# Two layers over a dense 8192 x 8192 adjacency on one core: x in another DMA queue, one-time work in other places, high and low G summed in the same columns

## The chip, the core and the metric

One core of a Trainium2 chip runs the program once. The metric is the device time in microseconds (us), from start to end of the program, lower is better. The engines are TensorE (PE), VectorE (DVE), ScalarE (ACT), GpSimd (POOL) and SyncE (SP); each works through its own list of instructions in order and waits on semaphores for the others. 16 DMA engines move data between HBM and the core's memory.

## What is computed

Two graph layers with a residual and a layer norm each, over N = 8192 nodes with F = 64 features. adj is a float32 matrix of 8192 x 8192 (268 MB) that holds only 0 and 1.

```python
def _L0_gnn_ref(X, adj, W, b):
    deg = jnp.clip(jnp.sum(adj, axis=1, keepdims=True) + 1.0, 1.0, None)
    h_neigh = (adj @ X + X) / deg
    z = jnp.concatenate([X, h_neigh], axis=1) @ W + b
    out = jax.nn.relu(z)
    norm = jnp.linalg.norm(out, axis=1, keepdims=True)
    return out / jnp.maximum(norm, 1e-12)

def _L1_gnn_ref(features, adj, W):
    deg = jnp.sum(adj, axis=1, keepdims=True)
    neigh = adj @ features / (deg + 1.0)
    return jnp.concatenate([features, neigh], axis=-1) @ W.T

x = _layernorm(x + _L0_gnn_ref(x, adj, L0_gnn_W, L0_gnn_b), axis=-1)
x = _layernorm(x + _L1_gnn_ref(x, adj, L1_gnn_W), axis=-1)
```

The second layer needs adj @ features, and these features are the first layer's result.

## The kernel before

**The stream.** adj is read once. It goes through in 64 row blocks n of 128 rows, each in four chunks c of 128 x 2048 float32 (1 MB). `a_in` has R = 6 buffers for them. SyncE issues chunk t = 4n + c as soon as VectorE (`s_e`) and ScalarE (`s_half`) are done with chunk t - 6. With each chunk:

- VectorE compares it with 1.0 into 8-bit codes `e8` (`compare`, L802).
- ScalarE sums the upper halves of its words, as a check that there are only zeros and ones (`sum_codes`, L589). The first use of ScalarE loads its table.
- TensorE multiplies the codes, as pairs in float16, with powers of two (`pack_chunk`, L371), which transposes them and packs eight rows' bits into a byte. ScalarE takes the packed bytes to `pk` (`take_packed`), GpSimd keeps copies in `store` (`keep`), VectorE unpacks them into `t_sb`, fp8 weights of 0 or 2 (`unpack`, L809).
- TensorE sums: for each of the 64 column blocks b, the weights `t_sb[b]` times a row of `xh`, into `s_ps` (`sum_quarter`, L385).

**What `xh` holds.** For each column block 257 columns in float16: g high (64) and g low (64), which are the first layer's results as two halves, x high (64), x low (64), and a constant for the degree (1). The columns of g are known only for the column blocks whose first layer is done. `lows(n)` says how many of these row block n uses: 0 up to row block 10, then 8, 16, 24, 32, 40 for eight row blocks each, 48 from row block 51 on. For b < lows(n) the matmul has all 257 columns, for the others the last 129. What a row block missed is made up from `store`: in pieces beside the stream (`unpack_piece`, `catch_up` L404, `add_piece`, from row block 12 on), and the last 16 column blocks for all rows after the stream (`unpack_tail`, `tail_sums` L466 and L470, `add_tail`).

**The first layer.** Every four row blocks (a group e) ScalarE has copied the sums into `agg` (`take_sums`, L609: 257 columns or 129). GpSimd adds x low to x high (`join_x`, L1186) and g low to g high (`join_g`), and copies the degrees to `dcol`. VectorE divides by the degree (`mean`, L847 and L851), and then come transposes, the dense product, `norm`, `residual`, `normalise`, the second dense product, `low_part` and `begin_acc`, over row blocks 4e + 5 to 4e + 7, on all engines in turn.

**One-time work.** x comes in four DMAs from ScalarE's queue (L577), behind the weights. `split_x(q)` makes a quarter of x high on ScalarE and of x low on VectorE, one after each chunk of row block 1. `weights()` (L765 to L780) and `bias()` (L785 to L794) run on VectorE at the end of row block 2. `guard_x(q)` (L759, L760) checks the squares of a quarter of x, in row blocks 3 to 6. `verdict()` uses them at the very end.

**The order** is written out by hand: each engine has one loop over n, in which the calls stand between the four chunks. VectorE's, shortened:

```python
for n in range(NB):
    compare(n, 0)
    if n: unpack(n - 1, 0)
    ...
    compare(n, 3)
    if n == 2:
        weights()
        bias()
    if 3 <= n < 7:
        guard_x(n - 3)
```

## Time and profile before

| | |
|---|---|
| median of 3 runs | 761.63 us (760.83 to 764.16) |
| the profiled execution | 762.74 us |
| its span, first to last instruction | 760.9 us |
| PE, DVE, ACT, POOL busy | 83%, 90%, 77%, 41% of the span |
| mean granted TensorE clock | 0.948 of full speed |
| read from HBM | 270.60 MB, 358 GB/s over the span |

A time in a row counts from the span's start. "Busy" is the time in which an engine works on an instruction; TensorE's matmuls overlap, so its busy share is no measure of its peak. The granted clock is TensorE's share of full speed: 1.00 is 2.4 GHz, 0.50 is 1.2 GHz, and a stretch between the two is a mixture. "Idle before <- releaser" says for what an engine waited. The chain is followed back from the last instruction, at each step to what released it. The DMA share is the mean of the 16 DMA engines.

### The profile page before, as it was taken

The page shows a single profiled execution, that of the slowest core. Times are in us where ns is not written, and L with a number is a line of the kernel's source. Part 1 is how long each engine was busy: PE and PEld are TensorE (multiplying, and loading weights), DVE is VectorE, ACT ScalarE, POOL GpSimd, SP SyncE. Part 2 cuts the span into 40 slices and gives each one's busy share as a digit, 9 for nine tenths or more (in the row PEclk, how much of TensorE's full clock was granted, in tenths as well). Part 3 has the DMA queues.
Part 4 walks back from the last instruction along what each step waited for, and adds up shares of the span by engine and source line. Part 5 has one row for each costly group of instructions (what it writes and reads, how often), then busy time and mean ns, then how long its engine had stood idle before and what let it go on. Part 6 is the DMA issues. An engine that isn't in the chain of part 4 may idle for free.

```text
span 760.9 us, 27768 instructions
## 1 busy us (share of the span) xinstructions
PE 630.8 (83%) x11125; PEld 580.0 (76%) x11125; DVE 682.1 (90%) x2506; ACT 588.8 (77%) x815; POOL 312.3 (41%) x360
## 2 busy tenths in 40 slices
PE   1357687687777778979899998999999999998994
PEld 0246677676776677878788887989898989988994
DVE  4499998989998999899999999999999999987895
ACT  1978879989898888989889898888898888850021
POOL 0233323433421425664354545556553546341025
PEclk9987877989999997999999999999999999999998
DMA  9999999999999999999999999999999999900003
GB/s 361 406 366 402 420 347 420 422 420 418 421 419 419 419 419 407 382 419 419 419 414 420 408 421 402 420 413 408 413 391 420 399 418 394 420 24 2 2 18 102
DMA packets 41516, 274.54 MB, mean 361 GB/s; under 512 B 4455, under 2 KB 8615, under 8 KB 8615
## 3 DMA queue, kind: packets, MB, share of 16 engines
q1 hardware_dynamic: 39040, 270.55, 87.1%
q10 hardware_dynamic: 2342, 2.16, 0.9%
q8 instruction: 90, 1.47, 0.8%
q14 instruction: 44, 0.35, 0.1%
HBM read 270.60 MB, written 2.10 MB: 358 GB/s over the span
## 4 chain that ended last, share of the span: by engine, by line
PE 31%; DVE 25%; issue 13%; ACT 11%; DMA 11%; POOL 7%; ACTq 2%; DVEq 0%; POOLq 0%; SPq 0%
PE s_ps L385 17%; DMA a_in<-in_adj 11%; ACT junk L589 8%; DVE e L802 7%; DVE t_sb L809 6%; PE u_ps L404 5%; POOL small L1179 4%; PE p_ps L371 2%; PE z_ps L454 2%; DVE q_sb L870 2%; DVE y_sb L864 2%; ACTq L577 2%; PE p_ps L466 1%; DVE a_in L809 1%; POOL store L1211 1%
## 5 line engine op out<-in xcount | busy, mean ns | idle before, releaser
L589 ACT ACTIVATE junk<-a_in 128x2048 uint8<-128x2048 uint16 x256 | 488.4, 1913 | 8.8 <-DMA a_in<-in_adj 8.6
L385 PE MATMUL s_ps<-xh,t_sb 128*128 128x129 f16 x4096 | 388.2, 251 | 52.3 <-DVE t_sb L809 48.8
L385 PEld LDWEIGHTS s_ps<-xh,t_sb 128*128 128x128 fp8e4 x4096 | 314.7, 103 | 81.3 <-DVE t_sb L809 53.8
L802 DVE TENSOR_SCALAR e<-a_in 128x2048 uint8<-128x2048 f32 x256 | 314.1, 1234 | 18.7 <-DMA a_in<-in_adj 17.9
L1211 POOL COPY store<-pk 128x32 uint32<-128x32 uint32 (+1 forms) x250 | 176.1, 746 | 179.9 <-ACT pk L598 179.9
L809 DVE TENSOR_SCALAR t_sb<-pk 128x128 uint32<-128x128 uint32 x1024 | 159.1, 227 | 5.6 <-ACT pk L598 4.8
L371 PE MATMUL p_ps<-pow_h,e 128*128 128x16 f16 x2048 | 90.8, 171 | 65.7 <-DVE e L802 55.0
L371 PEld LDWEIGHTS p_ps<-pow_h,e 128*128 128x128 f16 x2048 | 77.6, 99 | 79.9 <-DVE e L802 60.1
L1179 POOL TENSOR_TENSOR small<-small,minus_half 128x4 f32<-128x4 f32 x32 | 68.8, 2150 | 151.8 <-DVE small L858 104.9
L404 PE MATMUL u_ps<-xh,u_sb 128*128 128x64 f16 x2976 | 105.6, 192 | 0.0
L404 PEld LDWEIGHTS u_ps<-xh,u_sb 128*128 128x128 fp8e4 x2976 | 100.6, 97 | 1.2
L1186 POOL TENSOR_TENSOR agg<-agg 128x256 f32<-128x256 f32 x16 | 30.5, 1905 | 74.1 <-ACT agg L609 74.1
L809 DVE TENSOR_SCALAR u_sb<-store 128x128 uint32<-128x128 uint32 (+5 forms) x416 | 58.6, 213 | 0.0
L598 ACT ACTIVATE pk<-p_ps 128x256 uint16<-128x256 f32 x128 | 47.9, 374 | 9.1 <-PE p_ps L371 9.1
L589 ACT ACTIVATION_READ_ACCUMULATOR junk<-a_in 128x1 f32 x256 | 50.6, 198 | 0.0
L615 ACT COPY cat_t<-c_ps 128x512 f32<-128x512 f32 x16 | 9.4, 585 | 31.1 <-PE c_ps L418 31.1
L633 ACT COPY h_t<-c_ps 64x512 f32<-64x512 f32 x16 | 9.3, 579 | 29.1 <-PE c_ps L446 29.1
L1218 POOL TENSOR_TENSOR fvar<-fvar,minus_half 128x8 f32<-128x8 f32 x8 | 16.1, 2012 | 37.9 <-DVE fvar L940 37.1
L609 ACT COPY agg<-s_ps 128x257 f32<-128x257 f32 (+1 forms) x64 | 22.5, 352 | 6.6 <-PE s_ps L388 6.6
L809 DVE TENSOR_SCALAR a_in<-store 128x256 uint32<-128x256 uint32 x128 | 26.9, 285 | 0.0
L652 ACT ACTIVATE t_sb<-xl 128x512 f32<-128x512 f32 x7 | 4.4, 626 | 28.6 <-DVE xl L929 28.6
L639 ACT CAST xh<-z_ps 128x256 f16<-128x256 f32 x16 | 6.0, 372 | 22.2 <-PE z_ps L454 22.1
(119 smaller groups left out, 487.5 us busy)
## 6 DMA issues: line engine op xcount, KB each, us to landing
a_in<-in_adj SPq DMA_DIRECT2D x256, 1024.0 KB, 11.2
xl<-in_x ACTq DMA_DIRECT2D x4, 512.0 KB, 18.3
out_h<-e SPq DMA_DIRECT2D x8, 256.0 KB, 2.1
b_sb<-in_L_gnn_b ACTq DMA_DIRECT2D x3, 0.2 KB
w_sb<-in_L_gnn_W ACTq DMA_DIRECT2D x1, 32.0 KB
w_raw<-in_L_gnn_W ACTq DMA_DIRECT2D x1, 32.0 KB
```

The lines of the kernel that those rows point to most:

```text
L371: last = nc.tensor.matmul(p_ps[:, c // 2, at:at + PK], e_pair[:, c, u // 2, :, u % 2], pow_h[:, :], start=True, stop=True)
L385: last = nc.tensor.matmul(s_ps[:, n % 2, at:GW], t_sb[:, b // 2, b % 2::2], xh[:, b, at:GW], start=(b == 0), stop=False)
L404: last = nc.tensor.matmul(u_rows[:, r, 0:F], u_sb[:, (r * W + b) // 2, b % 2::2], xh[:, low(q - 1) + b, part * F:(part + 1) * F], start=(b ...
L589: nc.scalar.activation(junk[:, t % 2, :], halves[t % R], ACT.Copy, scale=1.0 / 128, accum_out=half_sum[:, n, c:c + 1]).then_inc(s_half, 1)
L598: nc.scalar.activation(pk_u[:, n % 2, h * 256:(h + 1) * 256], p_ps[:, h, 0:256], ACT.Copy, bias=-CODE_SUM, scale=1024.0).then_inc(s_pk, 1)
L609: nc.scalar.copy(agg[:, e % 2, k, at:GW], s_ps[:, n % 2, at:GW]).then_inc(s_agg, 1)
L802: nc.vector.tensor_scalar(e8[:, c, :], a_in[:, t % R, :], 1.0, float(CODE), ALU.is_equal, ALU.add).then_inc(s_e, 1)
L809: ins = nc.vector.tensor_scalar(plane(g), src, by, BIT4, op, ALU.bitwise_and)
L1179: nc.gpsimd.tensor_tensor(small[:, dst, :], small[:, src, :], minus_half[:, 0:BR], ALU.pow).then_inc(s_root, 1)
L1186: nc.gpsimd.tensor_tensor(hi, hi, lo, ALU.add).then_inc(s_xsum, 1)
L1211: ins = nc.gpsimd.tensor_copy(stored(s, n, 1), pk_w[:, n % 2, at:at + WIDTH[s] * PKW])
L1218: nc.gpsimd.tensor_tensor(fvar[:, 1, rows], fvar[:, 1, rows], minus_half[:, :], ALU.pow).then_inc(s_froot, 1)
```

## The change

- SyncE issues x, behind the four chunks of row block 0; ScalarE no longer does.
- ScalarE makes a copy of one column into `warm` before its first chunk; its table load goes there.
- `split_x` for all four quarters, and ScalarE's `take_weights`, stand ahead of row block 1's first chunk. `weights()` goes to the end of row block 1, `bias()` behind the second chunk of row block 0 (with a wait for the weight DMAs), the guards to row blocks 20, 24, 28 and 32.
- A known column block is summed by two matmuls with the same weights: g high (64 columns) into columns 0 to 63 of `s_ps`, then g low, x high, x low and degree (193 columns) into columns 0 to 192. So g high and g low add up in PSUM, and the sum is 193 columns wide instead of 257. The first column block takes three. `agg` and `take_sums` become narrower.
- GpSimd's `join_x` and `join_g` go. VectorE adds x low to x high in `mean`. GpSimd keeps the copy to `dcol` (`keep_degrees`). `begin_acc` no longer waits for it.

```diff
+GUARD = [20, 24, 28, 32]
...
+                if n == 0:
+                    for q in range(NC):
+                        sp.dma_start(x_in[:, q * CB:(q + 1) * CB, :].rearrange("p (j r) f -> p j (r f)", r=IL),
+                                     x_j[:, q * CB // IL:(q + 1) * CB // IL, :]).then_inc(s_x[q], 16)
...
                 for b in range(i * CB, (i + 1) * CB):
-                    at = 0 if b < lows(n) else HP
-                    last = nc.tensor.matmul(s_ps[:, n % 2, at:GW], t_sb[:, b // 2, b % 2::2], xh[:, b, at:GW],
-                                            start=(b == 0), stop=False)
+                    row_bits = t_sb[:, b // 2, b % 2::2]
+                    if b < lows(n):
+                        nc.tensor.matmul(s_ps[:, n % 2, 0:F], row_bits, g_hi[:, b, :], start=(b == 0), stop=False)
+                    if 0 < b < lows(n):
+                        last = nc.tensor.matmul(s_ps[:, n % 2, 0:SW], row_bits, xh[:, b, F:GW], start=False, stop=False)
+                        continue
+                    if b < lows(n):
+                        nc.tensor.matmul(s_ps[:, n % 2, 0:F], row_bits, g_lo[:, b, :], start=False, stop=False)
+                    last = nc.tensor.matmul(s_ps[:, n % 2, F:SW], row_bits, xh[:, b, HP:GW],
+                                            start=(b == 0 and not lows(n)), stop=False)
...
-            for q in range(NC):
-                act.dma_start(x_in[:, q * CB:(q + 1) * CB, :].rearrange("p (j r) f -> p j (r f)", r=IL),
-                              x_j[:, q * CB // IL:(q + 1) * CB // IL, :]).then_inc(s_x[q], 16)
+            act.wait_ge(s_const, 1)
+            nc.scalar.copy(warm[:, :], ident[:, 0:1])
...
-                at = 0 if lows(n) else HP
-                nc.scalar.copy(agg[:, e % 2, k, at:GW], s_ps[:, n % 2, at:GW]).then_inc(s_agg, 1)
+                at = 0 if lows(n) else F
+                nc.scalar.copy(agg[:, e % 2, k, at:SW], s_ps[:, n % 2, at:SW]).then_inc(s_agg, 1)
...
             def bias():
 
+                dve.wait_ge(s_w, 80)
...
-                dve.wait_ge(s_xsum, e + 1)
+                hi, lo = (agg[:, par, :, F + i * F:2 * F + i * F] for i in range(2))
+                link(nc.vector.tensor_tensor(hi, hi, lo, ALU.add))
...
-            def join_x(e):
+            def keep_degrees(e):
...
                 pool.wait_ge(s_agg, (e + 1) * BR)
-                hi, lo = (agg[:, e % 2, :, HP + i * F:HP + (i + 1) * F] for i in range(2))
-                nc.gpsimd.tensor_tensor(hi, hi, lo, ALU.add).then_inc(s_xsum, 1)
...
-                    nc.gpsimd.tensor_tensor(hi, hi, lo, ALU.add)
```

VectorE at the start of the program, before. L802 is a chunk's comparison, L752 a quarter of x low, L809 an unpacking of eight instructions, L765 the first instruction of the weights:

```order
L752 SCALAR_TENSOR_TENSOR xh<-xl,xh 128x16x64
L802 TENSOR_SCALAR e<-a_in 128x2048
L809 TENSOR_SCALAR t_sb<-pk 128x16x8 x8
L802 TENSOR_SCALAR e<-a_in 128x2048 x2
L809 TENSOR_SCALAR t_sb<-pk 128x16x8 x8
L802 TENSOR_SCALAR e<-a_in 128x2048
L765 TENSOR_TENSOR w_sb<-w_sb,ident 64x64
L766 TENSOR_REDUCE small<-w_sb 128x1
L767 TENSOR_SCALAR small<-small 128x1
L768 TENSOR_TENSOR w_sb<-w_sb,small 128x64
```

The same place in the changed kernel, where the lines are L811, L760 and L818. L803 is the last instruction of the bias, L773 the first of the weights:

```order
L803 CAST b_rows<-b_sum 3x256
L811 TENSOR_SCALAR e<-a_in 128x2048 x2
L760 SCALAR_TENSOR_TENSOR xh<-xl,xh 128x16x64 x4
L811 TENSOR_SCALAR e<-a_in 128x2048
L818 TENSOR_SCALAR t_sb<-pk 128x16x8 x8
L811 TENSOR_SCALAR e<-a_in 128x2048 x2
L818 TENSOR_SCALAR t_sb<-pk 128x16x8 x8
L811 TENSOR_SCALAR e<-a_in 128x2048
L773 TENSOR_TENSOR w_sb<-w_sb,ident 64x64
L774 TENSOR_REDUCE small<-w_sb 128x1
```

The bias now ends ahead of row block 0's last two comparisons, and the four quarters of x low stand together ahead of row block 1. The weights follow row block 1 instead of row block 2.

SyncE's first rows in the changed kernel (before, all 256 chunks stand in one row):

```order
L329 UNCONDITIONAL_BRANCH
L337 DMA a_in<-in_adj 128x2048 x4
L340 DMA xl<-in_x 128x4x256 x4
L337 DMA a_in<-in_adj 128x2048 x252
L348 DMA out_h<-e 128x2x256 x8
```

Four DMAs of x now stand between chunk 3 and chunk 4.

TensorE in row block 12, at the first sums that know g (row block 11, lows = 8), before. L371 packs a chunk, L385 sums:

```order
L385 MATMUL s_ps<-xh,t_sb 128x129 x16
L388 MATMUL s_ps<-xh,id 128x129
L371 MATMUL p_ps<-pow_h,e 128x16 x8
L385 MATMUL s_ps<-xh,t_sb 128x257 x8
L385 MATMUL s_ps<-xh,t_sb 128x129 x8
L371 MATMUL p_ps<-pow_h,e 128x16 x8
```

And in the changed kernel, the same place (L378 packs, L393 to L399 sum):

```order
L402 MATMUL s_ps<-xh,id 128x129
L378 MATMUL p_ps<-pow_h,e 128x16 x8
L393 MATMUL s_ps<-xh,t_sb 128x64
L398 MATMUL s_ps<-xh,t_sb 128x64
L399 MATMUL s_ps<-xh,t_sb 128x129
L393 MATMUL s_ps<-xh,t_sb 128x64
L395 MATMUL s_ps<-xh,t_sb 128x193
L393 MATMUL s_ps<-xh,t_sb 128x64
```

A matmul of 257 columns became one of 64 and one of 193, and the first of the row block three.

## Rows read from the trace of the kernel before

**Rows 1.** The page, part 2: DMA share and GB/s in 40 slices.

```profile
DMA  9999999999999999999999999999999999900003
GB/s 361 406 366 402 420 347 420 422 420 418 421 419 419 419 419 407 382 419 419 419 414 420 408 421 402 420 413 408 413 391 420 399 418 394 420 24 2 2 18 102
```

**Rows 2.** Waits of SyncE's own queue: who, for whom, us, times, longest.

```profile
SPq L333 <- ACT junk L589: 505.5, 243, 15.7
```

**Rows 3.** The line of SyncE's chunk issues (L334): from issue to landing.

```profile
DMA to landing us min/median/max: 4.7/11.2/16.8
```

**Rows 4.** Windows: length, busy us of each engine, granted clock, DMA share, GB/s.

```profile
52.00:58.00 6.00, 2.91 (x38) 2.82 (x39) 5.86 (x19) 0.48 (x4) 0.00 (x0) 0.50 0.70 249
58.00:66.00 8.00, 5.99 (x82) 5.73 (x80) 7.93 (x20) 8.00 (x11) 1.99 (x6) 0.71 1.05 420
66.00:70.00 4.00, 3.94 (x68) 3.77 (x66) 4.00 (x11) 3.12 (x5) 1.56 (x3) 0.77 0.89 324
70.00:96.00 26.00, 16.05 (x230) 14.61 (x227) 25.62 (x74) 21.31 (x31) 10.97 (x18) 0.85 1.01 422
96.00:116.00 20.00, 16.84 (x233) 15.50 (x234) 18.67 (x55) 15.99 (x21) 3.19 (x16) 0.77 0.98 350
...
120.00:300.00 180.00, 140.10 (x2249) 126.12 (x2248) 166.00 (x635) 160.23 (x218) 62.12 (x124) 0.91 1.01 418
300.00:490.00 190.00, 172.52 (x3131) 158.26 (x3130) 179.35 (x675) 166.10 (x226) 102.59 (x93) 0.98 1.01 413
```

**Rows 5.** The same for four row blocks near the stream's end.

```profile
615.00:656.00 41.00, 40.16 (x684) 36.57 (x682) 38.53 (x147) 35.49 (x49) 20.69 (x10) 1.00 1.00 407
```

**Rows 6.** The chain that ended last, 675:705: start, us, what.

```profile
679.32 6.27 PE s_ps L385 x64
...
686.11 3.75 PE u_ps L466 x64
689.86 0.44 PE c_ps L418 x4
690.30 3.57 PE p_ps L466 x64
```

**Rows 7.** Timeline of VectorE, 44:56: start, us, engine, line, operation.

```profile
45.64 0.21 DVE L765 TENSOR_TENSOR w_sb<-w_sb,ident 64x64 f32<-64x64 f32 x1
...
49.24 0.17 DVE L785 MEMSET ones_bf<- 3x128 bf16 x1
...
53.12 1.21 DVE L802 TENSOR_SCALAR e<-a_in 128x2048 uint8<-128x2048 f32 x1
```

**Rows 8.** Groups by line, VectorE, 20:130: the guards' two instructions.

```profile
L760 DVE TENSOR_REDUCE xsq<-store 128x16 f32<-128x1024 f32 x4 | 4.9, 1220 | 0.1
L759 DVE TENSOR_TENSOR store<-xl 128x1024 f32<-128x1024 f32 x4 | 4.8, 1211 | 0.0
```

**Rows 9.** Timeline of all engines, 0:20.

```profile
3.15 13.10 ACTq L577 DMA_DIRECT2D xl<-in_x  x4
...
5.86 1.23 DVE L802 TENSOR_SCALAR e<-a_in 128x2048 uint8<-128x2048 f32 x1 [1.78 <-DMA a_in<-in_adj]
...
16.29 1.28 ACT L589 ACT_TABLE_LOAD   x1 [16.29 <-issue]
...
17.58 1.91 ACT L589 ACTIVATE junk<-a_in 128x2048 uint8<-128x2048 uint16 x1
```

**Rows 10.** The chain that ended last, 629:640.

```profile
631.30 1.43 PE u_ps L404 x48
...
634.11 1.80 PE s_ps L385 x16
...
637.06 0.92 PE s_ps L385 x16
```

**Rows 11.** Timeline of GpSimd and VectorE, 648:655.

```profile
648.90 2.50 POOL L1186 TENSOR_TENSOR agg<-agg 128x256 f32<-128x256 f32 x1 [2.61 <-ACT agg L609]
...
651.50 0.43 DVE L851 TENSOR_TENSOR cat_in<-agg,small 128x256 f32<-128x256 f32 x1 [0.60 <-DVE small L847]
```

## What I expected before it ran

> **What bounds the kernel now.** I read the page first, then the share and rate of the DMA over the span, then windows of it, then the chain.
>
> The adjacency is 268 MB and has to come through once, so the first thing to see is the DMA line: it stands at 9 in 35 of 40 slices, and its GB/s line is about 420 in most of them but 366, 402, 347 and 383 in some [rows 1]. Until the last megabyte has landed the kernel can't end sooner than the stream lets it. So an engine that is made faster is worth nothing there, unless it was late enough to leave the queue empty. Only six chunks of a_in exist; SyncE sends the next one when VectorE and ScalarE are both done with the one six before, and a chunk takes 11.2 us from issue to landing in the median [rows 3], so there are normally more than four in the queue. SyncE's 505.5 us of waiting for ScalarE [rows 2] is therefore no loss in itself: that wait is how a full queue looks. A loss is a window in which the rate drops.
>
> The windows show where it does [rows 4]. From 120 to 300 us the rate is 418 GB/s, which I take as what the stream gives. It is 249 in 52:58, 324 in 66:70 and 350 in 96:116. The time lost is (418 - 249) / 418 x 6 = 2.4 us, (418 - 324) / 418 x 4 = 0.9 us and (418 - 350) / 418 x 20 = 3.3 us, 6.6 us together. Before 52 us there is a short dip while x itself comes, 2 MB in small packets, and these are still sent after the change. After 120 us nothing of this size is left.
>
> In the last third a second bound comes up beside the stream. In 615:656 TensorE is busy for 40.16 of 41 us, at the full granted clock, with the DMA still at 407 GB/s; VectorE is busy for 38.53 and ScalarE for 35.49 [rows 5]. The two bounds are level there. After the stream the end hangs on TensorE's sums of row block 63, then on its tail sums [rows 6].
>
> **The early edits: what they give.** The loss in 52:58 has one cause that the rows show. VectorE works on the weights from 45.64 and on the bias from 49.24, and takes its next chunk only at 53.12, so one-time work of 7.4 us stands between two chunks [rows 7]. Then come four guards of 1.21 + 1.22 = 2.43 us each, 9.7 us together, in row blocks 3 to 6 [rows 8]. VectorE is busy for 7.93 of 8 us in 58:66, for 4.00 of 4 in 66:70 and for 25.62 of 26 in 70:96 [rows 4]. It has no room to catch up: 17.1 us of one-time work lie where each microsecond makes TensorE and ScalarE late too.
>
> The change takes the bias (53.12 - 49.24 = 3.9 us) into row block 0, between the second chunk and the third. VectorE waits there for each chunk anyway (1.78 us before the first, [rows 9]), and has one comparison of 1.23 us to do in the 2.5 us of a chunk. The weights (3.6 us) go to the end of row block 1, and the guards to row blocks 20, 24, 28 and 32. VectorE is busy for 166.00 of 180 us in 120:300 and for 179.35 of 190 in 300:490 [rows 4]: 14.0 and 10.7 us are free, and two guards, 4.9 us, are put into each. A row block is four chunks of 2.5 us, and a guard makes one chunk 2.4 us late where there are four in the queue. So I cost the moved guards at nothing; the cover is the queue, and if it is gone each guard costs up to 2.4 us.
>
> ScalarE's early start goes the same way. Its issues of x held it until 16.25 us, then came the table load of 1.28 us, and its first chunk began at 17.58 though VectorE had taken it at 5.86 [rows 9]. After the change it takes chunk 0 as it lands, some 12 us earlier. In row block 1 both engines now wait for all of x before they take a chunk; in SyncE's queue x stands behind four chunks, so the last of its bytes moves at 1 + 6.3 MB / 0.418 = 16 us or, its packets being small, a few us later, and chunk 4 stands behind it. Both engines are therefore ready when chunk 4 lands. The copy into warm and the table load lie in idle time. The bytes are the same, so x itself gives and costs 0.
>
> How much of the 6.6 us comes back? The 2.4 and the 0.9 us follow VectorE's 17.1 us and I take them whole. In 96:116 the granted clock is 0.77, a mixture of the two levels, and TensorE is busy for 16.84 of 20 us [rows 4]: it slows down after it idled behind VectorE, and some of this belongs to the first dense stage and stays. Of the 3.3 us I take 1.9. Sum: **-5.2 us**. The bounds are -2.4 us (only 52:58 is mended) and -6.6 us (all of it).
>
> **The sums in the same columns.** A known column block of a row block was one matmul of 257 columns, and is now one of 64 and one of 193 with the same weights, loaded twice (for the first block three: 64, 64, 129). The chain gives what one takes in a row at full clock: 1.80 / 16 = 112.5 ns for 257 columns, 0.92 / 16 = 57.5 ns for 129, 1.43 / 48 = 29.8 ns for 64 [rows 10]. No row has 193; on the line between 129 and 257 it is 57.5 + 64 x 55 / 128 = 85.0 ns. The pair takes 114.8 ns, 2.3 more than before. lows(n) is 8, 16, 24, 32, 40 for eight row blocks each from 11 on, and 48 for the 13 row blocks from 51: 1584 pairs, 3.6 us of TensorE in all. Up to row block 50 the stream hides it. From 51 on TensorE and the stream are level, so 13 x 48 = 624 pairs stand on the path: 624 x 2.3 ns = **+1.4 us**, and the 13 first blocks add 13 x 5 ns = 0.1 us. Bounds: 0, if the 0.84 us in 41 that TensorE idles take it up [rows 5]; above, 55.8 ns (3.57 / 64) for the short one, as a matmul of 128 columns with its own weights takes [rows 6], so 26 ns more on each of 624, +16 us. I take the value of the 64-column row, because L404 does just this: two matmuls of 64 columns with the same weights one after the other, into the same columns.
>
> Here the Trainium skill speaks against the change. TensorE: Matmul & The Clock Gate, section Back-to-back issue gap, gives about 81 ns a matmul as the sustained rate of 128 columns with weight loads, because both operations set the spacing. By it a pair would take at least 162 ns. The rows have 55.8 ns for that shape [rows 6] and 29.8 ns for 64 columns [rows 10], so the trace does not agree, and the sum goes by the rows; with 162 ns the 624 pairs would cost 49.5 ns each, 31 us.
>
> **What this takes from the others.** GpSimd's join of x took 2.50 us in the stream; VectorE was idle for 0.60 us before L851, which needs it [rows 11]. Now VectorE adds 256 elements itself, about 0.43 us like L851, plus the link: 0.1 us less than the wait. GpSimd also loses the join of G; what is queued behind the two (keep, then root) only starts earlier, 0. ScalarE's copy of s_ps is 193 columns instead of 257, and ScalarE has 5.5 us free in 41 [rows 5]: 0. begin_acc loses its wait for dcol: 0. In the tail TensorE sums row block 63 in 6.27 us, 0.1 more with 48 pairs (counted above), and the shorter copy behind it gives 0.1 back; the earlier mean is swallowed, since TensorE's tail sums are in front of the transposes [rows 6].
>
> **Sum.** The profiled execution took 762.74 us, its span 760.9; the median of the runs is 761.63. Change: -5.2 + 1.5 - 0.1 for the mean = -3.8, less 0.2 kept for the waits on x in row block 1, so -3.6 us. Span 757.3, that execution 759.1, the median **758.0 us**. One can tell 0.5% (3.8 us) from no change here, and this is just under it.
>
> **Rivals.**
> *All of it comes back.* The late engines in 96:116 are only the echo of VectorE's 17.1 us, and TensorE's idle takes up the pairs: 761.6 - 6.6 = 755.0. For it: VectorE had no microsecond free from 58 to 96. Against: the clock of 0.77 in a stretch whose work stays. Chance 0.17.
> *The dips move.* Row blocks 4 to 9 stay irregular, the clock stays low, and only 52:58 is mended; TensorE pays at the end: -2.4 + 1.5 = -0.9, 760.7. Chance 0.18.
> *The short matmul pays for its weights.* Place: TensorE from row block 51, where it is level with the stream. It decides the sign at 5.2 us / 624 = 8 ns on a pair. At the upper bound of 28 ns it is +17.5 - 5.2 = +12.3, 774 us, and it would start earlier than row block 51, so rather more. For it: the weights of a short one have only 27 ns of columns to hide behind. Against: 29.8 ns on 48 in a row. Chance 0.10.
> *x in SyncE's queue does not do what it should.* ScalarE's four issues took 13.10 us [rows 9]. SyncE's may be held too, with chunks 4 and 5 behind it. At the least one quarter of x, 0.5 MB or 1.3 us, is then left to move, and a chunk lands 4.7 us after its issue at the least [rows 3], so up to 3.4 us would be lost: 761.4. Against: the queue holds six megabytes by then, and an issue is let through as packets end. Chance 0.06.
>
> **How the numbers follow.** The forecast has 0.49; it spans 755.5 to 760.5, and half of it lies under 757.8. Faster by over 0.5%: 0.25 + 0.17 = 0.42. Within: 0.24 + 0.18 + 0.06 + 0.02 of the short matmul's small prices = 0.50. Slower: 0.08. The range is 754.5 to 762.5: it takes in all but the short matmul's prices.
>
> **What would show it.** Windows of the changed kernel: 415 to 420 GB/s in each from 24 to 120 us, VectorE with idle time in 58:96, and no fall in 200:340, where the guards went (right); a dip of 250 or 350 left in 96:116 (second rival). The chain in the last 100 us: a 64 and a 193 matmul should start 115 ns apart from the next pair (right), 125 or more is the third rival. Row block 51 should come 5 us earlier than before, row block 63's sums 3.6 us earlier; if the first holds and the second doesn't, TensorE's price was mis-sized. The whole is wrong if the stream stops being the bound before row block 51.

## The result and the profile after

The changed kernel takes **772.64 us** in the median of its runs (771.15 to 773.74); the kernel before, run beside it, 762.59 (760.83 to 764.16). The ratio is 1.013, 95% interval 1.010 to 1.016: slower by 10 us, where I had forecast 758.0. The profiled span is 770.9, before 760.9.

The page of the changed kernel, part 2, DMA share and GB/s in 40 slices of 19.3 us, and its line of the instruction packets from part 3 (packets, MB, share of 16 engines):

```profile
DMA  9999999999999999999999999999999999900003
GB/s 346 420 422 419 420 417 421 418 421 415 420 419 419 416 408 397 418 402 403 411 403 408 397 420 403 392 372 369 380 405 390 396 387 392 379 8 2 3 18 99
...
q8 instruction: 102, 1.67, 0.9%
```

The beginning is what the change was for: no slice from the second to the fourteenth is under 415, where [rows 1] has 366, 402 and 347. The end is new: from slice 25 on the rate is 369 to 405, where before it was 391 to 420. The same in windows (length, busy us of PE, PEld, DVE, ACT, POOL with counts, granted clock, DMA share, GB/s), the first five against [rows 4]:

```profile
52.00:58.00 6.00, 4.64 (x78) 4.21 (x77) 3.54 (x10) 5.03 (x8) 0.00 (x0) 0.87 1.01 419
58.00:66.00 8.00, 4.97 (x71) 4.43 (x69) 6.49 (x20) 6.78 (x9) 2.48 (x8) 0.79 1.01 420
66.00:70.00 4.00, 2.23 (x43) 1.79 (x40) 2.74 (x7) 3.95 (x6) 2.05 (x7) 1.00 1.02 424
70.00:96.00 26.00, 21.55 (x255) 19.44 (x256) 23.00 (x83) 22.24 (x33) 11.63 (x18) 0.71 1.01 420
96.00:116.00 20.00, 13.66 (x207) 12.06 (x205) 15.87 (x48) 17.90 (x24) 3.74 (x16) 0.84 1.01 418
```

```profile
533.00:574.00 41.00, 39.24 (x854) 38.44 (x854) 36.82 (x139) 35.56 (x49) 19.33 (x10) 1.00 0.95 369
574.00:615.00 41.00, 40.15 (x840) 39.07 (x838) 37.43 (x147) 34.59 (x48) 16.43 (x8) 1.00 0.99 395
615.00:656.00 41.00, 38.50 (x829) 37.68 (x827) 35.73 (x135) 33.21 (x47) 16.76 (x8) 1.00 0.99 391
```

In the late windows no engine is busier than before. In 615:656 TensorE has 38.50 us of work where [rows 5] has 40.16, VectorE 35.73 for 38.53, ScalarE 33.21 for 35.49, and the stream is slower too. Everybody waits for somebody. The groups of TensorE in 492:656 say for whom; line, shape and count, busy us and mean ns, then the idle time before them and who ended it. First of the kernel before, then of the changed one:

```profile
L385 PE MATMUL s_ps<-xh,t_sb 128*128 128x257 f16 (+1 forms) x1018 | 107.7, 257 | 2.6 <-DVE t_sb L809 2.6
L404 PE MATMUL u_ps<-xh,u_sb 128*128 128x64 f16 x1200 | 41.1, 192 | 0.0
```

```profile
L395 PE MATMUL s_ps<-xh,t_sb 128*128 128x193 f16 x665 | 84.0, 247 | 1.1 <-issue 1.0
L393 PE MATMUL s_ps<-xh,t_sb 128*128 128x64 f16 x681 | 83.0, 193 | 2.2 <-DVE t_sb L818 1.2 <-issue 1.0
L418 PE MATMUL u_ps<-xh,u_sb 128*128 128x64 f16 x1136 | 39.3, 192 | 1.9 <-issue 1.8
L399 PE MATMUL s_ps<-xh,t_sb 128*128 128x129 f16 x304 | 23.5, 219 | 1.6 <-issue 1.6
```

Before, TensorE never stood still for "issue", that is with nothing to wait for in the profile. After the change it did for 5.4 us here. The timeline of TensorE shows what such a piece looks like:

```profile
530.99 0.62 PE L399 MATMUL s_ps<-xh,t_sb 128*128 128x129 f16 x8
531.45 1.21 PE L418 MATMUL u_ps<-xh,u_sb 128*128 128x64 f16 x35
534.04 0.55 PE L418 MATMUL u_ps<-xh,u_sb 128*128 128x64 f16 x13 [1.38 <-issue]
534.42 0.35 PE L378 MATMUL p_ps<-pow_h,e 128*128 128x16 f16 x8
```

48 matmuls of catch_up should run without a break: nothing is waited for between them, and before the change they took 1.43 us [rows 10]. Here 35 go, TensorE stands for 1.38 us, and 13 follow. The break is in the middle of a loop body whose operands were all there.

One more column of the trace fits it. The queue named "instruction" brings packets of 16 KB through the same 16 DMA engines as adj; there were 90, now there are 102. One of them started at 531.6, 0.9 us before that break. I counted the breaks of this kind between 120 and 690 us: two matmuls of one run (the same line, or the two lines of a pair) that start more than 330 ns apart. The kernel before has none. The changed kernel has 15, 13.8 us in all from start to start, and each begins 0.3 to 2.0 us after the start of an instruction packet, while such a packet starts every 6.2 us in 492:656. That made the first theory.

Where time was gained and lost, as the start of VectorE's comparison of a row block's first chunk against the kernel before (us, from the trace):

```
row block            12    28    36    44    48    52    56    60    63
changed kernel     -6.3  -7.1  -4.3  -2.4  -0.4  +3.7  +4.5  +6.3  +8.8
```

The chain that ended last has its last long piece of sums, then the tail, as in [rows 6]:

```profile
693.85 0.91 PE s_ps L399 x16
695.23 3.75 PE u_ps L480 x64
699.42 3.57 PE p_ps L480 x64
```

686.11 has become 695.23, 9.1 us later; the tail behind it has the same length to within 0.9 us.

### The profile page after: what moved, and what is told of

Its sections match the earlier page's. It is cut to its first block, busy times and chain, and to the rows that moved or that the text cites. A ratio compares the mean times of both kernels' runs of the same rounds, so it can differ in the third digit from the quotient of the medians.

```text
span 770.9 us, 31027 instructions
## 1 busy us (share of the span) xinstructions
PE 645.1 (84%) x12762; PEld 615.8 (80%) x12762; DVE 681.2 (88%) x2522; ACT 588.1 (76%) x816; POOL 290.6 (38%) x330
## 4 chain that ended last, share of the span: by engine, by line
PE 40%; DVE 21%; DMA 13%; issue 13%; ACT 7%; POOL 3%; SPq 1%; ACTq 0%; DVEq 0%; POOLq 0%
DMA a_in<-in_adj 13%; PE s_ps L395 11%; PE u_ps L418 7%; PE s_ps L399 6%; ACT junk L602 5%; DVE e L811 5%; DVE t_sb L818 5%; PE s_ps L393 5%; PE p_ps L378 3%; POOL small L1182 2%; PE z_ps L468 2%; DVE q_sb L880 2%; DVE y_sb L874 2%; PE p_ps L480 1%; DVE a_in L818 1%
## 5 line engine op out<-in xcount | busy, mean ns | idle before, releaser
L602 ACT ACTIVATE junk<-a_in 128x2048 uint8<-128x2048 uint16 x256 | 488.4, 1913 | 17.3 <-DMA a_in<-in_adj 17.0
L811 DVE TENSOR_SCALAR e<-a_in 128x2048 uint8<-128x2048 f32 x256 | 311.7, 1224 | 23.8 <-DMA a_in<-in_adj 23.0
L1205 POOL COPY store<-pk 128x32 uint32<-128x32 uint32 (+1 forms) x250 | 198.6, 836 | 228.9 <-ACT pk L611 228.9
L399 PE MATMUL s_ps<-xh,t_sb 128*128 128x129 f16 x2565 | 204.9, 235 | 23.5 <-DVE t_sb L818 19.4
L393 PE MATMUL s_ps<-xh,t_sb 128*128 128x64 f16 x1584 | 200.2, 196 | 18.9 <-DVE t_sb L818 14.7
L395 PE MATMUL s_ps<-xh,t_sb 128*128 128x193 f16 x1531 | 200.1, 252 | 1.1 <-issue 1.0
L399 PEld LDWEIGHTS s_ps<-xh,t_sb 128*128 128x128 fp8e4 x2565 | 171.6, 105 | 26.3 <-DVE t_sb L818 21.9
L393 PEld LDWEIGHTS s_ps<-xh,t_sb 128*128 128x128 fp8e4 x1584 | 153.0, 99 | 21.5 <-DVE t_sb L818 16.6
L818 DVE TENSOR_SCALAR t_sb<-pk 128x128 uint32<-128x128 uint32 x1024 | 152.2, 222 | 5.5 <-ACT pk L611 4.7
L395 PEld LDWEIGHTS s_ps<-xh,t_sb 128*128 128x128 fp8e4 x1531 | 153.0, 100 | 2.1 <-issue 1.3
L378 PE MATMUL p_ps<-pow_h,e 128*128 128x16 f16 x2048 | 91.6, 171 | 65.5 <-DVE e L811 61.8
L1182 POOL TENSOR_TENSOR small<-small,minus_half 128x4 f32<-128x4 f32 x32 | 65.9, 2060 | 200.8 <-DVE small L868 152.1
L378 PEld LDWEIGHTS p_ps<-pow_h,e 128*128 128x128 f16 x2048 | 77.6, 99 | 79.2 <-DVE e L811 68.8
L818 DVE TENSOR_SCALAR u_sb<-store 128x128 uint32<-128x128 uint32 (+5 forms) x416 | 59.7, 218 | 0.0
L849 DVE TENSOR_TENSOR xl<-u_ps,xl 128x256 f32<-128x256 f32 (+5 forms) x52 | 20.3, 391 | 10.0 <-PE u_ps L418 10.0
```

The lines of the kernel that those rows point to most:

```text
L378: last = nc.tensor.matmul(p_ps[:, c // 2, at:at + PK], e_pair[:, c, u // 2, :, u % 2], pow_h[:, :], start=True, stop=True)
L393: nc.tensor.matmul(s_ps[:, n % 2, 0:F], row_bits, g_hi[:, b, :], start=(b == 0), stop=False)
L395: last = nc.tensor.matmul(s_ps[:, n % 2, 0:SW], row_bits, xh[:, b, F:GW], start=False, stop=False)
L399: last = nc.tensor.matmul(s_ps[:, n % 2, F:SW], row_bits, xh[:, b, HP:GW], start=(b == 0 and not lows(n)), stop=False)
L602: nc.scalar.activation(junk[:, t % 2, :], halves[t % R], ACT.Copy, scale=1.0 / 128, accum_out=half_sum[:, n, c:c + 1]).then_inc(s_half, 1)
L811: nc.vector.tensor_scalar(e8[:, c, :], a_in[:, t % R, :], 1.0, float(CODE), ALU.is_equal, ALU.add).then_inc(s_e, 1)
```

## The experiments

**Theory A:** TensorE runs out of instructions; with more of them per microsecond, its packets come too late beside the stream. **Theory B:** the second matmul of a pair costs because it adds into columns that the one ahead has just written. A third candidate was the early edits themselves. I split the change in two and took 1488 matmuls away in another place.

**The early edits alone.** The changed kernel with the sums, agg and the joins as they were before; against the changed kernel:

```diff
-                    if b < lows(n):
-                        nc.tensor.matmul(s_ps[:, n % 2, 0:F], row_bits, g_hi[:, b, :], start=(b == 0), stop=False)
-                    if 0 < b < lows(n):
-                        last = nc.tensor.matmul(s_ps[:, n % 2, 0:SW], row_bits, xh[:, b, F:GW], start=False, stop=False)
...
+                    last = nc.tensor.matmul(s_ps[:, n % 2, at:GW], t_sb[:, b // 2, b % 2::2], xh[:, b, at:GW],
+                                            start=(b == 0), stop=False)
```

> The kernel before with the early edits alone (x's loads in SyncE's queue, warm-up of ScalarE, splits of x before the compares, guards and bias moved); sums as before: one matmul of 257 columns per known row block, joins on GpSimd. The kernel before has a median of 762.6 us, the changed one 772.6. Theory A (TensorE runs short of instructions: the loss comes with the number of its instructions) and theory B (the loss comes from adding into columns that the matmul ahead has just written) both say that the early gain stays: 757 us (756 to 758.5), since in the changed kernel chunk (13,0) landed 5.9 us and chunk (40,0) 5.8 us earlier than before. If the early edits are what spoils the late row blocks (the rival here), it is 762 or more.

760.26 us (757.71 to 763.23), ratio 0.997 [0.9952, 0.9989], span 757.9. The rule for breaks finds one pause of 0.4 us, at 131 us; it lies 11 us behind a packet and so is of another kind.

**The same-column sums alone.** The other half of the change; against the changed kernel:

```diff
-GUARD = [20, 24, 28, 32]
...
-                        split_x(q)
-                    take_weights()
...
+                if n == 1:
+                    split_x(0)
...
+                if 3 <= n < 7:
+                    guard_x(n - 3)
```

> The kernel before with the same-column sums alone (64 + 193 columns, joins moved from GpSimd to VectorE); the early part as before. If the two halves of the change add up, its time is the changed kernel's plus the early gain: 772.6 + 5.5 = 778 us (775 to 780). If the loss only exists because the stream of adj runs ahead by 5 us, it is 763 to 767.

772.35 us (771.23 to 774.55), ratio 1.0128 [1.0103, 1.0153], span 771.1, with 15 breaks, 11.4 us (one of them, 0.4 us at 138 us, is 11 us behind a packet). So the loss comes with the sums, and the two halves do not add up: the early edits are worth 2 to 3 us by themselves and nothing beside the sums. My 778 took the early gain for 5.5 us at the end; with 2.4 us, what the early edits give alone, it would have been 775, and the rest of the miss is that the halves do not add up.

**Fewer matmuls in catch_up.** In the changed kernel:

```diff
-                        for part in range(2):
-                            last = nc.tensor.matmul(u_rows[:, r, 0:F], u_sb[...], xh[:, low(q - 1) + b, part * F:(part + 1) * F],
-                                                    start=(b + part == 0), stop=(b + part == W))
+                        last = nc.tensor.matmul(u_rows[:, r, :], u_sb[...], xh[:, low(q - 1) + b, 0:HP],
+                                                start=(b == 0), stop=(b == W - 1))
...
+                link(nc.vector.tensor_tensor(rows, u_rows[:, 0:r1 - r0, 0:F], rows, ALU.add))
+                nc.vector.tensor_tensor(rows, u_rows[:, 0:r1 - r0, F:HP], rows, ALU.add).then_inc(s_uadd, 1)
```

> The changed kernel with the products of the stored codes merged: one matmul of 128 columns (high and low part side by side) in place of two of 64 columns that add up in the same columns, and one more addition on VectorE per row block from 12 on. 1488 matmuls and as many weight loads fewer. The main sums keep their same-column form. Theory A: the gaps of TensorE that wait for nothing fall from 15 us to under 6, and with two of 64 columns at 31.5 ns each giving way to one at 57.5 it comes to 760 us (757 to 764). Theory B as far as the main sums go: their pairs cost what they did, the merged ones save 5.5 ns x 1488 = 8 us of TensorE at most: 765 to 768 us, gaps as in the changed kernel.

768.51 us (767.26 to 770.01), ratio 1.0073 [1.0051, 1.0095]. The breaks are gone: none between 120 and 690, with 8709 matmuls there, the main sums still in their pairs into the same columns. That speaks for A. The time only fell by 4 us, and A had promised 12. The likely reason, VectorE, comes further down.

**The same number of instructions, no column written twice.** In the kernel with the early edits alone:

```diff
+                    row_bits = t_sb[:, b // 2, b % 2::2]
                     at = 0 if b < lows(n) else HP
-                    last = nc.tensor.matmul(s_ps[:, n % 2, at:GW], t_sb[:, b // 2, b % 2::2], xh[:, b, at:GW],
-                                            start=(b == 0), stop=False)
+                    if b < lows(n):
+                        nc.tensor.matmul(s_ps[:, n % 2, 0:HP], row_bits, xh[:, b, 0:HP], start=(b == 0), stop=False)
+                        at = HP
+                    last = nc.tensor.matmul(s_ps[:, n % 2, at:GW], row_bits, xh[:, b, at:GW],
+                                            start=(b == 0 and not lows(n)), stop=False)
```

> e1_early (760.3 us; 757.9 in its profiled span) with each 257-column matmul of a known row block sent as two, of 128 and 129 columns, that write different columns: as many instructions on TensorE as the changed kernel, no column written twice; ScalarE, VectorE and GpSimd as in e1_early. Theory A (TensorE runs short of instructions above some rate): gaps over 330 ns inside runs of one line, 11 to 14 us of them between 120 and 690 (changed kernel 13.8, early edits alone 0.4), each 1 to 2 us behind a packet of the instruction queue, and 770 us (767 to 774). Theory B (adding into columns just written costs): no such gaps, 760 to 763 us.

769.21 us (768.35 to 770.0), ratio 1.0091 [1.0074, 1.0108], 13 breaks, 9.6 us, each 1.1 to 2.3 us behind a packet's start. Theory B had 760 to 763. It falls: 9 of the 12 us between the early edits alone and the changed kernel are there without a column that is written twice. TensorE's groups of this kernel in 492:656:

```profile
L396 PE MATMUL s_ps<-xh,t_sb 128*128 128x129 f16 x986 | 105.5, 220 | 2.2 <-issue 2.2
L394 PE MATMUL s_ps<-xh,t_sb 128*128 128x128 f16 x699 | 86.2, 219 | 1.5 <-DVE t_sb L815 1.4
L415 PE MATMUL u_ps<-xh,u_sb 128*128 128x64 f16 x1136 | 39.3, 192 | 0.8 <-issue 0.7
```

**Half the dose.** The same with `if b < lows(n) and b % 2:`.

> e3_split2 with the odd column blocks alone split: half the extra instructions. About 9450 matmuls between 120 and 690 beside 8700 (early edits alone; no gaps) and 10150 (changed kernel; 13.8 us of gaps). Theory A in its form with a threshold (packets of 16 KB that come at their own pace): fewer than 5 us of gaps and a span of 760 to 763; if the loss is in proportion to the instructions: 6 to 7 us of gaps and a span of 764. Theory B: no gaps, span 758 to 759.

One execution: span 760.0, 9451 matmuls between 120 and 690, one break of 0.3 us. The breaks are no straight line in the number of matmuls: half of the extra ones bring 0.3 us, all of them 9.6. In the span the first half costs 2.1 us and the second 7.5, but that is from one execution each, and two executions of the early edits alone differ by 2.4 us. In 492:656 the rates are

```
                       matmuls per us   breaks in 120:690   span
before                      17.3              0             760.9
half split                  19.3              0.3           760.0
all split                   20.8              9.6           767.5
changed kernel              20.7             13.8           770.9
```

**Instructions without a matmul.** In the kernel of the early edits with early guards (below), ahead of each matmul of 257 columns:

```diff
+                    if b < lows(n):
+                        for ready, value in ((s_w, 80), (s_b0, 1), (s_w1, 1)):
+                            pe.wait_ge(ready, value)
```

> e6_guard (759.0 us) with two or three more instructions ahead of each known row block's matmul of 257 columns: waits on semaphores (weights, bias) that have stood at their values since row block 3. No matmul, no weight load and no column more than in e6_guard; in instructions it is as much as the changed kernel or more. Theory A: gaps inside runs of matmuls 1 to 2 us behind an instruction packet, 5 us of them or more, and 766 to 775 us. If what costs is the extra matmul and weight load themselves: 759 to 761 us and no gaps.

767.93 us (765.07 to 771.15), ratio 1.0068 [1.0046, 1.0089], against 759.0 without the waits, where the trace has one break, of 0.7 us. TensorE has the same 11125 matmuls; the trace has 1902 semaphore instructions on its queue where there were 291. There are 12 breaks, 9.6 us, each 0.9 to 2.0 us behind a packet's start. So breaks come without one more matmul or weight load. They are not all that the waits cost: where one matmul of 257 columns follows another in 500:660, they start 122.5 ns apart in the mean and 111.8 ns without the waits, 6.8 us over 635 of them, and the two breaks among these are 1.7 us of it. The rest is 4 ns on the ordinary ones and 31 shorter pauses of 130 to 330 ns, most of them over 2 us behind a packet. How much of the 9 us the breaks are, this run does not separate. And one thing does not fit a mere count: these are 1611 instructions, as many as the half dose, with 96 packets in both kernels, at 16.5 matmuls per microsecond where the half dose has 19.3, and the half dose had one short break where this kernel has 12. Why a wait should be dearer for TensorE's supply than an instruction that works, no run here shows.

**The stream at half its rate.** In the changed kernel:

```diff
+THIN = 40
...
+                    part = CH if n < THIN else CH // 2
-                    sp.dma_start(a_in[:, t % R, :], adj_j[n // IL, n % IL, :, c * CH:(c + 1) * CH]).then_inc(s_in[t % R], 16)
+                    sp.dma_start(a_in[:, t % R, 0:part],
+                                 adj_j[n // IL, n % IL, :, c * CH:c * CH + part]).then_inc(s_in[t % R], 16)
```

> The changed kernel with only the first half (1024 of 2048 columns) of each chunk of adj loaded from row block 40 on; the other half of the buffer keeps an earlier chunk's numbers, so these sums are of other data, and every engine's instructions are as before. It asks whether TensorE's gaps come from the instruction packets' sharing the DMA engines with the stream. If they do (theory A1), packets take well under the 0.9 to 1.1 us that they take in the changed kernel and the gaps between 500 and 660 fall to under 2 us, period of four row blocks 41.5 us or less. If the packets come too late by themselves, at the rate at which TensorE uses them up (theory A2), gaps per row block stay within a third of those of the changed kernel. The theory of the starved stream (late chunks hold TensorE up) says no gaps and 41 us.

Its numbers are of other data, so it is no kernel to keep, and it ran once. Span 758.9, 12.0 less. Windows and TensorE's groups in 492:656:

```profile
533.00:574.00 41.00, 40.29 (x885) 39.52 (x883) 38.53 (x148) 34.64 (x47) 18.40 (x11) 1.00 0.69 199
615.00:656.00 41.00, 40.36 (x870) 39.59 (x868) 38.28 (x147) 34.72 (x49) 18.75 (x8) 1.00 0.69 206
```

```profile
L398 PE MATMUL s_ps<-xh,t_sb 128*128 128x193 f16 x678 | 85.1, 247 | 0.0
L396 PE MATMUL s_ps<-xh,t_sb 128*128 128x64 f16 x695 | 84.4, 192 | 1.9 <-DVE t_sb L821 1.8
L421 PE MATMUL u_ps<-xh,u_sb 128*128 128x64 f16 x1189 | 40.7, 192 | 0.0
L402 PE MATMUL s_ps<-xh,t_sb 128*128 128x129 f16 x320 | 24.3, 219 | 0.0
```

All of TensorE's instructions are there, at 21.5 matmuls per microsecond, more than in any other run, and no idle time before "issue" is left in these groups; the last break of the run is at 413 us, before the first halved chunk landed (420.3). With the DMA engines at a share of 0.69 the packets come in time. The packets themselves took as long as ever (median 0.96 us in 500:656, 0.97 in the changed kernel), so if something got shorter, it lies ahead of them, and that the trace does not show.

The same cut in a kernel with next to no breaks, the one with the early edits and early guards, is the control:

> e6_guard (span 757.8) with only the first half of each chunk of adj loaded from row block 40 on, as in e8_thin; the sums there are of other data. The control for e8_thin, in which the same cut took the changed kernel from a span of 770.9 to 758.9. If the halved stream helps through TensorE's instruction packets alone, e6_guard, which has no such gaps, gains under 1 us: 757. If it speeds something else up (buffers, VectorE's reads), it gains as well: 750 to 755, and that much of the 12 us of e8_thin is not the packets'.

Span 757.5 against 757.8. Half the stream is worth 0.3 us where TensorE has next to no breaks. So the 12 us of the run above came with the breaks, and the late stream of the changed kernel was their result and not the cause. The two halved kernels also bound the price of everything else in the sums (pairs, VectorE's addition, the joins): 758.9 - 757.5 = 1.4 us, from one execution each, of kernels that have their guards in different places, and so no firmer than the 2.4 us between two executions of one kernel.

**The addition of x on VectorE.** In the kernel of the early edits:

```diff
-                dve.wait_ge(s_xsum, e + 1)
+                hi, lo = (agg[:, par, :, HP + i * F:HP + (i + 1) * F] for i in range(2))
+                link(nc.vector.tensor_tensor(hi, hi, lo, ALU.add))
...
-                nc.gpsimd.tensor_tensor(hi, hi, lo, ALU.add).then_inc(s_xsum, 1)
```

> e1_early with the sum of x's high and low part on VectorE (one more instruction of 0.43 us per four row blocks, as in the changed kernel) in place of GpSimd, matmuls as before. If VectorE's extra 16 x 0.43 = 6.9 us counts in full where VectorE is 95% busy: 764 to 766 us. If TensorE alone is the bound: 760 us, as e1_early. Between them, with the wait for GpSimd gone that the row on cat_in shows (4.5 us in 200 to 600 of e1_early): 760 to 762, my value 761.

760.53 us (758.18 to 762.17), ratio 0.9977 [0.9962, 0.9993]: the same as without, within the noise. The addition of x is no part of the loss that these runs can tell.

**Fewer matmuls on top of the early edits.** The merged catch_up from above:

> e6_guard (759.0 us) with the products of the stored codes merged: one matmul of 128 columns in place of two of 64, which takes 1488 matmuls off TensorE, and one more addition of about 0.40 us on VectorE per row block from 12 on (52 x 0.40 = 21 us). In the traces two of 64 columns take 2 x 29.9 ns and one of 128 columns 55.9 ns. If TensorE alone is the bound from row block 36 on: 28 of 52 row blocks' share of 1488 x 3.9 ns = 5.8 us, 3 us less: 756 us. If VectorE, busy 95 of 100 us there, becomes the bound with the additions: 761 to 764 us; my value 762. A theory by which any instruction less on TensorE shortens the kernel, gaps or not, says 756 or less too.

769.56 us (768.25 to 771.21), ratio 1.0083 [1.0056, 1.0111]. I had 762, with VectorE as the new bound; it is that, and more of it. No break behind a packet (the one pause that the rule finds, 0.4 us at 135 us, is 14 us behind one), and the windows have VectorE at the top:

```profile
533.00:574.00 41.00, 38.84 (x556) 35.17 (x553) 40.14 (x148) 35.69 (x49) 8.59 (x12) 1.00 1.00 389
574.00:615.00 41.00, 39.00 (x525) 35.10 (x526) 39.70 (x146) 34.06 (x49) 6.97 (x10) 1.00 0.99 395
```

16 additions more in 492:656 take 7.4 us (0.46 each, as the row block's other one), 52 of them 20 us in all, and 10.6 us came out at the end though TensorE had less to do. VectorE had so little idle time left that it became the bound, as I had said, but at 10.6 us and not at the 3 that I had put on it. The same additions are the likely reason why removing the breaks with this edit gave only 4 us; the run does not prove it, but in its windows VectorE is busy for 39.6 to 40.1 of 41 us.

**The guards.** In the kernel of the early edits:

```diff
-GUARD = [20, 24, 28, 32]
+GUARD = [4, 6, 8, 10]
```

> e1_early with the four guards on x at row blocks 4, 6, 8, 10 in place of 20, 24, 28, 32. They are 8 VectorE instructions of 1.22 us, 9.8 us in all. In e1_early VectorE is busy 96 of 100 us between 200 and 400 and only 66.6 of 82 between 28 and 110; its lead over the kernel before shrinks there from 6 to 7 us (row blocks 12 to 28) to 3.6 us (row blocks 36 to 63). Theory C (the moved guards, set among work that fills VectorE, took 3 us of the early gain): 757.3 us (756 to 758.5). Rival (TensorE is the bound from row block 32 on and no shift of VectorE's work matters): 760.3 us.

758.97 us (758.66 to 759.58), ratio 0.9956 [0.994, 0.9973]. It beats the kernel before and the changed one. Its trace has one break, 0.7 us at 526 us and 1.8 us behind a packet. To tell it from the early edits with late guards I ran both again, on one chip:

> e1_early once more, beside e6_guard on the same chip. Theory C (the guards took 1 us or more of the early gain where VectorE is full): 1 to 3 us slower than e6_guard, 760 against 759 or less. Rival (TensorE's pace from row block 36 on sets the end, whatever the guards do): within 0.5 us of it.

> e6_guard once more, with more rounds, beside e11_early_again: the early edits with the guards at row blocks 4 to 10. 759.0 us (758 to 760), ratio to the kernel before 0.9955 with an upper end under 0.998.

759.7 us (757.28 to 761.48) with late guards, ratio 0.9966 [0.9948, 0.9983]; 758.48 (758.19 to 760.42) with early ones, ratio 0.9959 [0.9945, 0.9972]. The intervals lie over each other. The profiled run of the late guards this time had a span of 755.5, the shortest of all profiled ones, and that of the early ones 758.6. So I can't say that the late guards cost anything. What the traces do show is where the lead gets fixed. Comparison of a row block's first chunk against the kernel before, two profiled runs of each:

```
row block               12    28    36    44    52    63     span
late guards, first    -6.0  -7.0  -3.7  -3.4  -3.6  -3.5    757.9
late guards, second   -5.7  -8.2  -6.0  -5.4  -5.4  -5.4    755.5
early guards, first   -4.2  -8.6  -6.3  -5.2  -4.5  -4.5    757.8
early guards, second  -3.1  -8.8  -5.2  -3.4  -3.6  -3.6    758.6
```

After row block 44 nothing moves by more than 0.7 us. From there on all four keep the pace of the kernel before, with TensorE busy for 40.1 or 40.2 of 41 us in 574:615 and 615:656, and whatever lead is left by then is the gain. Between 250 and 350 us the first run of the late guards had TensorE at a granted clock of 0.90 and 0.93 of full (a mixture of its two levels), the second at 1.00 and 1.00; that goes with the 2 us between them, but one pair of runs does not prove it.

## Why the prediction was wrong

**The early edits, -5.2 us.** In the stream this step came true, by a little more: chunk (13, 0) landed 5.9 us earlier, (40, 0) 5.8 us, all windows from 24 to 120 us at 418 to 424 GB/s, VectorE with idle time in 58:96, 414 GB/s in 200:340 where the guards went. What failed is the step from the stream to the end. Alone, these edits gave 2.1 and 2.6 us of median and, in one profiled execution each, 3.0 and 5.4 of span. I had written that the stream and TensorE are level from row block 51; the table above has the lead frozen from row block 36 to 44 on. Between row blocks 28 and 44 each of the four executions loses 2.8 to 5.4 us of a lead of 7.0 to 8.8. With a bound that close behind the stream, the stream's gain can bring only the lead that the engines follow.

**The pairs, +1.4 us.** The price of a pair was too low. In 500:660 a 64 starts 32 ns and the next 64 another 85 or 86 ns after it (medians, 118 ns a pair). The mean over pairs without a break is 116.3 ns, where I had 114.8 and where 257 columns take 111.8: 4.5 ns more, not 2.3. The split into 128 and 129 columns has the same 116.2 ns, so the price belongs to any pair and the shared columns add 0.1 ns at most. 1584 pairs at 4.5 ns are 7 us of TensorE. With the breaks nearly gone, all that the sums added to the span was 1.4 us; that this is the number I had forecast is luck, as it is one execution against one. The Trainium skill's 81 ns per matmul (TensorE: Matmul & The Clock Gate, section Back-to-back issue gap) is for 128 columns and would make an estimate of 162 ns for a pair; the trace disagrees here too, 116.3 ns with breaks left out, and 56 ns for a matmul of 128 columns in a row.

**What was missing.** The term that decided the result is in none of my cases: 13.8 us of breaks. The changed kernel's profiled span is 13.0 us above that of the early edits alone. The step that failed is the sentence that a pair costs what its columns take "because L404 does just this". 48 short matmuls in a row did run at 29.8 ns before the change, where 17.3 matmuls per microsecond were needed on the whole and no break shows in the trace. I read a burst and priced a steady rate by it. The page had the row: the "instruction" queue, 90 packets of 16 KB on the same DMA engines that the stream keeps full. The number of TensorE's instructions (22250 with the weight loads, 25524 after) was there to be counted too. I never asked who brings the instructions.

**The rivals.** "The short matmul pays for its weights" had 774 us and the measurement is 772.6, but not by its mechanism, so the near hit is luck: it wanted 125 ns or more between pairs, and it is 118. It is right about one thing, that TensorE decides the sign from before row block 51. "Up to row block 50 the stream hides it" was wrong by the rows: of the 15.9 us that were lost between row blocks 28 and 63, 10.8 were gone by row block 52; against the early edits alone, which lose 3.5 of these by themselves, it is 7.3 of 12.3. x in SyncE's queue held SyncE for 8.5 us, so chunk 4 landed at 21.8 us and not at 17.3 as before, but chunk 12 is level again (43.2 against 43.0), and the cost of 0 stands. ScalarE's early start and the tail were as expected. The 383 GB/s that I read in [rows 1] is 382; nothing hangs on it. The last sentence of the prediction named the condition under which all of it fails, that the stream stops being the bound before row block 51, and that is what happened.

## What to carry to other kernels

Count instructions per microsecond, not only columns: a matmul with its weights is two instructions, they come in packets over the DMA engines, and on a kernel that streams at full rate TensorE can stop in the middle of a loop. Here there was at most one break behind a packet up to 19.3 matmuls per microsecond and 13 or more from 20.6 on. It is no fixed limit: with waits between the matmuls there were 12 at 16.5. Its mark is idle time before "issue" inside a run of equal matmuls, just behind a packet of the instruction queue; look at that before blaming columns, banks or weights. And a gain in the stream is worth only the lead that the second bound can follow: ask from which point the other engines are level, and take the lead there.

## What the runs showed of the hardware

Instruction packets of 16 KB, one for some 128 matmuls with their weight loads, run beside the stream. With the DMA engines at a share of 0.99 the changed kernel lost 13.8 us in 15 breaks behind such packets; with 0.69 it had not one (the three that are left, 1.9 us, lie at 309, 401 and 413 us, before the first halved chunk landed at 420.3). That the breaks come so suddenly (0.3 us at 19.3 matmuls per microsecond, 9.6 at 20.8) I had not expected, nor that 1611 waits which were long fulfilled would cost 9 us on a kernel of 760. A matmul of 64 columns followed by one of 193 with the same weights takes 116.3 ns in the mean, 4.5 more than one of 257; 128 and 129 columns, which share none, take 116.2.
